# The load of K into its slots, cut into 16-row transfers, with the first three slots filled apart

## What is computed

```
x = ln(x + attn_block(x))          # pre-norm attention, then a pre-norm MLP (256 -> 1024 -> 256, exact gelu)
x = ln(x + ffn(x))                 # top-1 of 8 experts: relu(x @ wi.T + wi_b + lora_e) @ wo.T + wo_b

def attn_block(x):                 # 16 heads of 16
    q, k, v = split(ln1(x) @ w_in.T + b_in)
    scores = q @ k.T / 4
    allowed = (row % 8 == 0) or (row == column)      # only every eighth query sees all keys
    o = softmax(where(allowed, scores, -inf)) @ v
    x = x + o @ w_out.T + b_out
    return x + gelu(ln2(x) @ w1.T + b1) @ w2.T + b2
```

## Time and profile before

| what | value |
|---|---|
| median of 3 runs | 1767.41 us (1760.43 to 1771.22) |
| the profiled execution | 1780.16 us, span 1778.3 us |
| PE busy | 1524.5 us (86%) |
| DVE, ACT, POOL busy | 48%, 41%, 37% |
| granted TensorE clock, mean | 0.927 |
| queue q1 (SP's), share of 16 engines' span | 22.7% |

### The profile page before, as it was taken

The page is one execution under the profiler, slowest core; times in us unless marked ns, Lnnn a source line. Parts: engine busy times, 40 slices in busy tenths (PEclk is TensorE's granted clock), DMA queues, the critical chain, the costliest instruction groups (busy, mean ns, idle before and its releaser), DMA issues.

```text
span 1778.3 us, 26328 instructions
## 1 busy us (share of the span) xinstructions
PE 1524.5 (86%) x10166; PEld 1117.7 (63%) x10166; DVE 858.9 (48%) x1786; ACT 730.5 (41%) x1071; POOL 652.4 (37%) x536
## 2 busy tenths in 40 slices
PE   5685977889876998899987999899986999889876
PEld 4574744557765865556876865556875775555765
DVE  5643545445634545553744645543662555444221
ACT  3241444444432454345333454445342354444432
POOL 1452320034653431224862431313762442213443
PEclk8897989899998999899998998889998999899988
DMA  6542101012532101110543111110552201010100
GB/s 161 172 146 93 44 21 64 28 49 74 188 108 90 66 33 44 53 45 31 190 145 107 41 52 40 50 48 22 166 166 92 72 31 64 26 60 13 48 13 12
DMA packets 101501, 132.06 MB, mean 74 GB/s; under 512 B 17417, under 2 KB 77777, under 8 KB 98257
## 3 DMA queue, kind: packets, MB, share of 16 engines
q1 hardware_dynamic: 101376, 130.38, 22.7%
HBM read 68.87 MB, written 61.36 MB: 73 GB/s over the span
## 4 chain that ended last, share of the span: by engine, by line
PE 52%; DMA 20%; SPq 9%; DVE 9%; POOL 3%; ACT 3%; issue 2%; POOLq 0%; DVEq 0%; ACTq 0%
DMA kslot<-k_d 15%; PE ps L1366 13%; PE ps L1367 10%; PE ps L1368 10%; PE ps L1542 5%; DMA x1in<-x_d 4%; PE ps L1531 4%; SPq L784 4%; PE ps L1516 3%; SPq L779 2%; SPq L781 2%; DVE xn L1242 2%; PE ps L1578 1%; POOL rows L918 1%; PE ps L1587 1%
## 5 line engine op out<-in xcount | busy, mean ns | idle before, releaser
L1279 DVE TENSOR_REDUCE mx<-ps 128x2 f32<-128x1024 f32 x256 | 313.2, 1223 | 348.4 <-PE ps L1516 347.5
L1029 ACT ACTIVATE prob<-ps 128x1024 f32<-128x1024 f32 x256 | 262.2, 1024 | 266.8 <-PE ps L1531 266.7
L1516 PE MATMUL ps<-kslot,qslot 48*128 48x512 f32 x512 | 119.8, 463 | 107.4 <-DMA kslot<-k_d 61.3
L927 POOL TENSOR_TENSOR hid0l<-gel,hid0h 128x512 fp32r<-128x512 f32 x86 | 111.8, 1300 | 251.8 <-ACT hid0h L1071 251.8
L927 POOL TENSOR_TENSOR hid2l<-gel,hid2h 128x512 fp32r<-128x512 f32 x85 | 110.5, 1300 | 246.0 <-ACT hid2h L1071 246.0
L927 POOL TENSOR_TENSOR hid1l<-gel,hid1h 128x512 fp32r<-128x512 f32 x85 | 110.6, 1301 | 241.4 <-ACT hid1h L1071 241.4
L1063 ACT ACTIVATE gel<-ps,cols 128x512 f32<-128x512 f32 x128 | 88.2, 689 | 257.7 <-PE ps L1368 210.6
L1542 PE MATMUL ps<-prob,vals 128*32 128x256 f32 x2048 | 171.4, 408 | 2.2 <-ACT prob L1029 2.2
L1065 ACT ACTIVATE gel<-ps 128x512 f32<-128x512 f32 x128 | 76.4, 597 | 150.9 <-PE ps L1606 149.2
L1531 PE MATMUL ps<-qslot,kslot 50*128 50x256 f32 x1024 | 133.3, 340 | 3.6 <-ACT prob L1029 3.6
L1531 PEld LDWEIGHTS ps<-qslot,kslot 50*128 50x128 f32 x1024 | 79.3, 192 | 85.2 <-issue 59.1
(11 more groups left out here) (230 smaller groups left out, 4077.6 us busy)
## 6 DMA issues: line engine op xcount, KB each, us to landing
k_d<-kst SPq DMA_DIRECT2D x96, 256.0 KB, 2.6
kslot<-k_d SPq DMA_DIRECT2D x64, 384.0 KB
xin<-in_L_attn_x SPq DMA_DIRECT2D x32, 256.0 KB, 3.8
x1in<-x_d SPq DMA_DIRECT2D x16, 512.0 KB, 5.1
rows<-xs_d SPq DMA_DIRECT2D x16, 512.0 KB, 5.3
out<-rows SPq DMA_DIRECT2D x16, 512.0 KB, 4.3
y_d<-rows SPq DMA_DIRECT2D x15, 512.0 KB, 3.1
rows<-y_d SPq DMA_DIRECT2D x15, 512.0 KB, 4.1
```

The costliest lines, as they stand in the source:

```text
L927: nc.gpsimd.tensor_tensor(hid[i % RING][1][:], gel[i % 2][:], hid[i % RING][0][:], ALU.subtract).then_inc(lo_done, 1)
L1029: nc.scalar.activation(prob[(n - 1) % 2][:].rearrange("p e i q -> p (e i q)"), ps[:, 0:2, :].rearrange("p a n -> p (a n)"), ACT.Exp).then_ ...
L1279: nc.vector.tensor_reduce(best[:, :, j % NQ], ps[:, MX:MX + 2, :], AX.X, ALU.max).then_inc(maxr_done, 1)
L1516: last = mm(ps[:, MX + e, :], qslot[p % SLOTS][half, P * t:P * t + P], kslot[p % SLOTS][half, 512 * piece:512 * piece + 512], start=True, ...
```

## The change

The 48 rows of K of one head go into the slot in three transfers, one for each copy, 16 rows each, where one transfer took all three. The counts on the slot's semaphore follow (from 96 to 160 for a first filling, from 64 to 128 after). And of the first three slots of a batch the second and the third are filled two and four items later than the first, so other steps of SP's queue come between them. The bytes moved are the same. The transfers of Q and of the ones stay as they are.

```diff
-                if j == ended + 2:
-                    for p in range(SLOTS):
-                        put(("kld", b, p))
+                if j in (ended + 2, ended + 4, ended + 6):
+                    put(("kld", b, (j - ended) // 2 - 1))
...
-        KCP[_k] += 96 if _s[2] < SLOTS else 64
+        KCP[_k] += 160 if _s[2] < SLOTS else 128
...
                         sp.dma_start(qslot[i][HALF * e:HALF * e + HROWS, :].bitcast(F32),
                                      q_d[:, HD * head:HD * head + HD, :]).then_inc(kcp[i], 16)
-                        sp.dma_start(kslot[i][HALF * e:HALF * e + HROWS, :].bitcast(F32),
-                                     k_d[:, HD * head:HD * head + HD, :]).then_inc(kcp[i], 16)
+                        for blk in range(3):
+                            at = HALF * e + HD * blk
+                            sp.dma_start(kslot[i][at:at + HD, :].bitcast(F32),
+                                         k_d[blk, HD * head:HD * head + HD, :]).then_inc(kcp[i], 16)
                         if p < SLOTS:
                             sp.dma_start(kslot[i][HALF * e + HROWS:HALF * e + SROWS, :].bitcast(F32), ones_d).then_inc(kcp[i], 16)
```

## The result

The changed kernel takes 1615.19 us, median of 3 runs (1611.93 to 1617.21), against 1767.41 before. The ratio is 0.9142, 95% interval 0.9090 to 0.9193. The profiled execution took 1617.21 us with a span of 1615.4; the span is 162.9 us shorter than before. The forecast was 1591 with a range of 1568 to 1642.

What follows compares the result with a forecast made beforehand. PE was taken to be held by slow loads of K on three engines and what queued behind them. 61.3 + 67.4 + 48 = 176.7 us off 1780.16 is 1603.5, less 12.75 gives 1591 us, range 1568 to 1642.

Steps and rivals of the forecast that it cites:

- Three engines: Load of K into the slots: the old transfer, three copies outermost, uses three of 16 DMA engines; the new gets 16.
- Term 1: K in 16-row transfers, in attention: a slot takes 9.3 us, so all 17 PE waits go, 61.3 us.
- Term 2: First fillings of each batch: PE's waits for the ones and for `hid` behind `x1in` nearly all go, 67.4 us.
- `x1in` lands with 5.1 us: In the fillings: the load of `x1in` lands 5.1 us after its issue on SP's queue.
- Term 3: Low granted clock after PE's waits: 122 us at half clock go, at 0.39 each, 48 us.
- DVE's waits: PE's five waits on the maxima from DVE, 7.6 us, were left standing in the forecast.
- the last step: From profiled execution to median: 12.75 us, by which the profiled execution lies above the median, were taken off 1603.5.
- (b): SP's issues bound the fillings, and late waits of batches 1 to 3 are 6 us each; 1611 us, chance 0.06.
- (a): PE's waits go but the clock still falls as much; 1639 us, chance 0.14 in full or half.
- (c): 16-row transfers use few engines or destination rows hold them up, a slot takes some 15 us; 1615 us, chance 0.07.
- (d): Slower: each transfer's landing is served alone, 20.8 us for a slot; 1844 us, chance 0.03.
- (e): Something other than the engine count limits K, such as HBM reads, so waits stay; 1805 us, chance 0.04.

Runs made afterwards that it cites:

- e4: Kernel before with slots filled two items apart and k_d, q_d laid out row outermost, copies inside, so one 48-row K transfer a head; 1602.18 us, ratio 0.9119.
- e5: Changed kernel with slot fillings from pair 3 on waiting for a later score step, so PE waits for K again; 1751.88 us, ratio 0.9888.
- e6: Changed kernel with the third slot filled one item later, behind the load of x1in in batches 1 to 3 too; 1602.42 us, ratio 0.9043.
- e8: e4 with a head's K cut into four transfers of 512 columns each; 1601.24 us, ratio 0.9040.
- e3: Changed kernel with a head's K in three transfers cut by columns, each with the three copies outermost; 1689.78 us, ratio 0.9621.
- e9: Kernel before with k_d stored in four padded stretches, so pieces are 2 KB, transfers otherwise as they were; 1822.20 us, ratio 1.0352.

## Why the forecast held, and where it was off

The forecast's direction and mechanism were right. By its steps:

- Three engines: right. Row order alone (e4) brings what the split brings.
- Term 1, 61.3 us: right, all 17 waits went. Two of its sub-steps were wrong and in part cancelled, which was luck. Issues are 0.54 us each, not 0.78, so the eighth starts 3.9 us after the first and not 5.5; but the last transfer lands some 7 us later and not 3.8, with the engines at about half the rate assumed. A slot takes 10.0 to 11.1 us (e5), not 9.3. The shortest time that PE left was 11.92 us after (pair 5 of batch 0, 255.35 to 267.27), so 1 us was to spare, not 2.3.
- Term 2, 67.4 us: 23.1 of 23.3 for the first waits and 37.6 of 47.05 for the late ones, 60.7 in all. The mis-sized value is 1 us left per batch, which measured 3.1. The step that failed is "`x1in` lands with 5.1 us". It was issued 5 us sooner than reckoned (21.4 us after the batch's first issue, 437.56 to 459.00, not 26.5), and then took 12.7 us behind two slots. The forecast took the landing from a median of loads with nothing ahead of them.
- Term 3, 48 us: PE busy fell by 47.2, and e5 gave it back from the other side. The product was nearer than its factors. By the mean clocks 2 x 0.073 x 1778.3 = 260 us of the span were at half clock before and 2 x 0.033 x 1615.4 = 107 after, PE's idle time included. That is 153 us less, where the forecast counted 122, and so 0.31 us each, not 0.39.
- DVE's waits, left at 7.6 us, measured 10.3; and 3.6 us of small gaps are not assigned.
- These make 6.7, 2.7, 0.8 and 3.6, the 13.8 us by which the profiled span fell short of 176.7. The forecast of the median lies 24.5 us below the result; the other 10.7 us lie in the last step, the 12.75 us by which the profiled execution stood above the median, where the changed kernel's stands 2.0 above its own. Savings counted in a slow execution were taken off the median. In one later series the executions of the kernel before run from 1751.73 us at a clock of 0.930 to 1776.04 at 0.921, those of the changed kernel from 1611.93 to 1617.21, so part of the spread went with what the change took away; how much is not shown.
- Of the forecast's signs, two did not come: DVE's wait for `x1in` is 22.6 us, not below 15, and an issue of K takes some 0.5 us, not 0.7. The late waits of batches 1 to 3 are 3.4 us at the longest, below the 5 us that would have spoken for (b), though 9.4 together.
- Rivals: (a) refuted by e5. (b) has the right place, SP's queue before `x1in`; but it is the drain and not a longer issue that made `x1in` late against the forecast. (c) has 1615, the measured time, and that is a coincidence: it asked for 15 us a slot and waits for K in batch 0, and a slot takes 10.0 to 11.1 us and no wait for K is left. Its idea that the rows hold the engines up is in part borne out, by the rate. (d) and (e) did not come.
- The Trainium skill's rule on merging small transfers, "DMA: Bandwidth & Descriptors", section "Rules for kernel authors", is no obstacle here, as PE waits for none of the small transfers; e4's large one gave as good a time with half the issues. The fit behind the forecast's 18.0 us is given on that page for transfers that GpSimd issues, and these are SP's; a slot takes 10.0 to 11.1 us.
- The Trainium skill's rule on the number of engines, "DMA: Bandwidth & Descriptors", section "Why a DMA increments its semaphore by 16 and not by 1", is borne out on both sides: the packet counts fit 3 engines before, and 16 in e4 and the changed kernel.

## What to carry over

Before cutting a transfer, look at its outermost dimension: the DMA share in a window that it fills alone, times 16, says about how many engines it has, and a change of layout can give all 16 to one large transfer. Price a PE wait that goes with the low clock behind it: here 2.4 us on top of waits of 3 to 7 us. And take the landing of a load from what stands ahead of it in the queue, not from its median; here moving one filling behind the load (e6) was worth 12 us more. And the added time of packets is no measure of how fast a load is: compare what is moved, or the time from first issue to use.

## Not expected

The packets of one slot took 74 to 86 us added up on sixteen engines and 47 on three, for the same 864 KB, so sixteen engines halved the time of a slot and did not bring it to a fifth. Stretches of 512 columns brought the sum down to 48 to 50, and the rate stayed (188 GB/s in e8, 204 in e4). On three engines the cut by columns did help (38 engine-us, e3), while pieces of 2 KB in unchanged row order made the kernel 3.5% slower (e9) at an unchanged 47; neither is explained. The issue of a 16-row transfer takes SP 0.4 to 0.5 us mostly, that of the three-copy one 0.7.
